# Convolutional attention kernel: attention product kept apart from the output projection

## The chip, the cores and the metric

The kernel runs on one NeuronCore of a Trainium2 chip. The metric is device time in microseconds of one execution. The kernel before takes 750.94 us (median of 3 runs, 750.56 to 751.97).

## The reference, cut to what matters

The input x is (4, 96, 56, 56) in FP32. An attention block and a mixture of four experts are each added to it. Attention has no softmax, so the sum over samples can be done ahead of the queries, as the kernel does; an image has 12 heads of 32 rows.

```python
x = x + conv_attention(layernorm_over_channels(x))
#   value, query: depthwise 3x3, stride 1      key, off: depthwise 3x3, stride 2 (784 places)
#   offset = w_off2 @ gelu(ln(off));  pos = tanh(offset + ref)
#   v_sampled = bilinear sample of value at pos       (784 samples, 96 channels)
#   query, key, v_sampled viewed as (B*NH, HC, pixels) with NH = 12, HC = 32
attn = einsum('bcm,bcn->bmn', query, key) * SCALE
out  = einsum('bmn,bcn->bcm', attn, v_sampled).reshape(B, C, H, W)
y    = einsum('bchw,oc->bohw', out, w_out)
t = tokens(x);  t = t + moe(ln(t))     # 4 experts of 96 -> 384 -> 96, exact gelu, best 2 gates
```

In code the reshape to 12 heads of 32 rows takes 8 channels of 96 for each head and cuts the 3136 pixels of a channel into 4 quarters of 784 (head row = channel in head x 4 + quarter, as it stands in memory). So "channel" means here a pair of a real channel and a quarter, and the 784 samples and keys are cut in the same way: keys have 196 places a quarter.

## The kernel before

Channels are laid on 128 partitions as 4 quarters x 32 channels, in three blocks (BLOCKS = 3, CB = 32): `val`, `query`, `key` and `off` are [128, 3, pixels of a quarter]. The four images go one after the other through a chain. Convolutions are taps on DVE (`tap`, L1133; part of image 0 on PE, L578). Value tokens are stored to a table in memory, POOL gathers sampled rows from it with 16 indirect DMAs an image (`gather`, L1469), and DVE weighs them into `vs` (`sample`, L1335 and L1338). Then comes the part in question.

`key_values` (L632) multiplies samples and keys, one quarter of samples at a time, into [96, 4 x 96]; it waits for one quarter of `vs` each. `mask_kv` (L1348) keeps the entries whose two channels are in the same head. `mixes` (L642) multiplies each masked part by `wout`, three products of 96 columns a quarter; ACT evacuates them to `mix`, [128, 4 quarters, 3 blocks, 96]. `attended` (L662) makes the output, already projected, in 8 steps of 392 pixels: each is three products of `mix` by `query`, summed in PSUM. `add_y` (L1354) on DVE adds it to x. After step n, PE turns x1 of step n-2 to tokens (`x1_to_tokens`, L650), ACT copies them (L826), DVE takes their statistics (`bn`), and the normed tokens go back to channels (`x1_back`, L511) for the experts.

Expert work is cut into chunks of 128 hidden units and 448 pixels, 84 an image, 336 in all. A chunk is three products of FP32R into `ph` (L762 to L764), GELU on ACT (L1006) and one FP32 product into `py` (L746). Three chunks make one output, which DVE scales by its gate into one of four `ye` slots (L1416). POOL issues a DMA that adds it to x for the first 76 (L1480) and adds the later ones itself (L1482); a slot is free when its sum is done. The last 84 chunks are run apart (`last_experts`), with split FP32R products.

The order on each engine is fixed by tables written out by hand or by a planner ahead of time. `CHUNKS_AHEAD` says how many chunks PE has issued before each step of an image, `GELUS_AHEAD` the same for ACT, `OUTPUTS_AHEAD` how many outputs DVE has made at each turn, and `SUMS_AHEAD` how many sums POOL has issued before each of the 8 pairs of gathers. PE, ACT, DVE and POOL run their own instructions strictly in that order. PSUM has two banks for work that ACT evacuates (`pa`) and two for DVE (`pd`); `act_jobs` and `dve_jobs` list their uses in order, and a bank is used again when the job two places before is done.

Of the kernel before, what the change touches and what calls it, by code (L numbers as in the profile page):

```python
# [33 lines left out]
NG = NT // GRP  # L34
# [34 lines left out]
def act_jobs():  # L69

    order = jobs(0, "xT", NG) + jobs(0, "pad", 2 * BLOCKS) + jobs(0, "offT", 2) + jobs(0, "valT", QT)[:VALUE_HALF] + jobs(0, "offc", 2) + jobs(0, "valT", QT)[VALUE_HALF:]
    order += jobs(1, "xT", NG)[:EARLY_SLOTS] + jobs(0, "keyT", 2) + jobs(1, "xT", NG)[EARLY_SLOTS:] + jobs(0, "mix", QUARTERS) + jobs(0, "x1T", NG) + jobs(1, "pad", 2 * BLOCKS)
    order += jobs(0, "gateT", 1) + jobs(1, "offT", 2) + jobs(1, "offc", 2)
    for b in range(1, BATCH):
        more = b + 1 < BATCH
        order += jobs(b, "valT", QT)
        if more:
            order += jobs(b + 1, "xT", NG)
        order += jobs(b, "keyT", 2)
        if more:  # L80
            order += jobs(b + 1, "pad", 2 * BLOCKS)
        order += jobs(b, "mix", QUARTERS) + jobs(b, "x1T", NG)
        if more:
            order += jobs(b + 1, "offT", 2)
        order += jobs(b, "gateT", 1)
        if more:
            order += jobs(b + 1, "offc", 2)
# [27 lines left out]
SCALE_AFTER = 4  # L115
# [3 lines left out]
    dict(x1c=(0, 0, 0, 0, 3, 3, 4), gateT=(3,), offT=(10, 10), offc=(16, 16), offs=(18,)),  # L119
    dict(valT=(42, 42, 43, 43, 44, 44, 45), xT=(45, 46, 46, 47, 47, 48, 48), keyT=(49, 49),  # L120
         pad=(69, 69, 70, 71, 71, 72), kv=(72, 72, 73, 73), mix=(73, 73, 74, 74), y=(74, 74, 74, 74, 74, 74, 74, 74),
         x1T=(74, 74, 74, 74, 74, 74, 75), offT=(75, 76), x1c=(80, 80, 81, 82, 86, 86, 87), gateT=(86,), offc=(93, 93),
         offs=(95,)),
    dict(valT=(118, 118, 119, 119, 120, 120, 121), xT=(121, 122, 122, 123, 123, 124, 124), keyT=(125, 125),
         pad=(145, 145, 146, 147, 147, 148), kv=(148, 148, 151, 151), mix=(151, 151, 152, 152),
         y=(152, 152, 152, 152, 152, 152, 152, 152), x1T=(152, 152, 152, 152, 152, 152, 153), offT=(153, 154),
         x1c=(158, 158, 159, 160, 164, 164, 165), gateT=(164,), offc=(172, 172), offs=(174,)),
    dict(valT=(198, 198, 199, 199, 200, 200, 201), keyT=(204, 204), kv=(222, 226, 233, 233), mix=(233, 233, 234, 234),
         y=(234, 234, 234, 234, 234, 234, 234, 234), x1T=(234, 234, 234, 234, 234, 234, 235),
         x1c=(241, 241, 243, 243, 249, 249, 250), gateT=(249,)),  # L130
# [3 lines left out]
    dict(x1n=(0, 0, 0), x1c=(0, 0, 0, 0, 3, 3, 4), exp=(0,), gateT=(3,), offT=(10, 10), offc=(16, 17), tanh=(19,)),  # L134
    dict(valT=(42, 42, 43, 43, 44, 44, 45), xT=(45, 46, 46, 47, 47, 48, 48), keyT=(49, 49), xn=(67, 69, 69),
         pad=(69, 70, 70, 71, 71, 72), mix=(73, 73, 74, 74), x1T=(74, 74, 74, 74, 74, 74, 75), offT=(75, 76),
         x1n=(78, 80, 82), x1c=(80, 81, 83, 84, 86, 86, 87), exp=(81,), gateT=(86,), offc=(93, 94), tanh=(95,)),
    dict(valT=(118, 118, 119, 119, 120, 120, 121), xT=(121, 122, 122, 123, 123, 124, 124), keyT=(125, 125),
         xn=(143, 144, 145), pad=(145, 146, 146, 147, 147, 148), mix=(151, 151, 152, 152),
         x1T=(152, 152, 152, 152, 152, 152, 153), offT=(153, 154), x1n=(156, 158, 160),  # L140
         x1c=(158, 159, 161, 162, 164, 164, 165), exp=(159,), gateT=(164,), offc=(172, 173), tanh=(175,)),
    dict(valT=(198, 198, 199, 199, 200, 200, 201), keyT=(204, 204), mix=(233, 233, 234, 234),
         x1T=(234, 234, 234, 234, 234, 234, 235), x1n=(239, 241, 243), x1c=(241, 242, 245, 245, 249, 249, 250),
         exp=(243,), gateT=(249,)),
# [43 lines left out]
def build(nc, t, out):  # L188
# [4 lines left out]
    with ExitStack() as ctx:  # L193
# [624 lines left out]
        def _(act):  # L818
# [133 lines left out]
            def first_rest(b, plan, gelus_to):  # L952
# [585 lines left out]
```

## Time and profile before

| | |
|---|---|
| median of the runs | 750.94 us (750.56 to 751.97) |
| profiled execution, span from first to last instruction | 749.4 us; the page gives no other time of it |
| PE busy | 707.8 us, 94% |
| weight loads busy (beside PE) | 495.8 us, 66% |
| DVE busy | 582.8 us, 78% |
| ACT busy | 384.5 us, 51% |
| POOL busy | 216.9 us, 29% |

A product's time in the groups of the page runs from its start to its modelled end, and consecutive products overlap. So the pace of products is read from the chain of waits or from the starts in the timeline, not from their mean. L numbers are lines of the kernel before.

### The profile page before, as it was taken

To read this page: it belongs to the slowest core of one execution; us is meant where nothing else is said; L and a number is where in the kernel's file an instruction comes from. 1 tells how busy PE (TensorE), PEld (TensorE's weight loads), DVE (VectorE), ACT (ScalarE), POOL (GpSimd) and SP (SyncE) were. 2 spreads that over 40 slices of the span, in tenths; PEclk is the share of its full clock that TensorE was granted. 3 is DMA by queue.
4 is the path that set the end of the run, shared out by engine and by line. 5 is a ranking of instruction groups with operands and counts; after the bars stand their busy time and mean duration, and the time that the engine had idled before them with its cause. 6 is when DMAs were issued, how large, how long until landed. Compare 5 with 4: busy or idle time off the path is not lost.

```text
span 749.4 us, 9619 instructions
## 1 busy us (share of the span) xinstructions
PE 707.8 (94%) x3186; PEld 495.8 (66%) x3186; DVE 582.8 (78%) x1511; ACT 384.5 (51%) x722; POOL 216.9 (29%) x184
## 2 busy tenths in 40 slices
PE   5798999799999999999999999999998999999996
PEld 5556566566676666556767566666664665788884
DVE  4889648899999858699999477899975275677774
ACT  2314124744464614744556218545542256899995
POOL 4001700012128610111168201222285121344443
PEclk9998999799999999999999999999999999999999
DMA  8007200044464530345654422435645201121111
GB/s 195 9 0 198 53 9 1 7 98 86 89 185 115 98 56 10 68 103 119 155 129 83 86 48 46 82 80 101 190 102 109 35 20 49 47 69 51 66 47 37
DMA packets 29697, 58.66 MB, mean 78 GB/s; under 512 B 6224, under 2 KB 20176, under 8 KB 29360
## 3 DMA queue, kind: packets, MB, share of 16 engines
q0 software_dynamic: 11584, 17.90, 15.4%
q1 hardware_dynamic: 14336, 32.59, 14.7%
q10 hardware_dynamic: 3728, 7.55, 3.3%
q8 instruction: 26, 0.43, 0.2%
q14 instruction: 23, 0.19, 0.1%
HBM read 30.30 MB, written 14.65 MB: 60 GB/s over the span
## 4 chain that ended last, share of the span: by engine, by line
PE 56%; DVE 19%; DMA 7%; ACT 6%; POOL 5%; issue 5%; POOLq 0%; ACTq 0%
PE py L746 9%; PE pd L662 8%; PE ph L578 7%; DVE val L1133 6%; POOL big L1469 4%; DMA xbuf<-ye 4%; DVE query L1133 3%; PE pa L650 3%; PE pa L529 2%; PE ph L762 2%; PE ph L782 2%; PE ph L784 2%; PE ph L763 2%; PE ph L783 2%; PE ph L764 2%
## 5 line engine op out<-in xcount | busy, mean ns | idle before, releaser
L746 PE MATMUL py<-hid,w 128*96 128x448 f32 x504 | 234.4, 546 | 11.5 <-ACT hid L1006 8.7
L1006 ACT ACTIVATE hid<-ph,b 128x448 f32<-128x448 f32 x252 | 158.9, 632 | 148.1 <-PE ph L764 144.8
L762 PE MATMUL ph<-x_hi,w_hi 96*128 96x448 f32 x252 | 164.4, 653 | 0.0
L1480 POOL DMA_DIRECT2D xbuf<-ye x76 | 66.6, 877 | 327.2 <-DMA xbuf<-ye 163.2
L1469 POOL DMA_INDIRECT big<-value_table,rows x64 | 87.8, 1372 | 90.5 <-DVE rows L1193 56.5
L746 PEld LDWEIGHTS py<-hid,w 128*96 128x96 f32 x504 | 81.6, 165 | 31.2 <-ACT hid L1006 12.6
L763 PE MATMUL ph<-x_lo,w_hi 96*128 96x448 f32 x252 | 93.5, 371 | 0.0
L764 PE MATMUL ph<-x_hi,w_lo 96*128 96x448 f32 x252 | 92.8, 368 | 0.0
L1482 POOL TENSOR_TENSOR xbuf<-xbuf,ye 96x448 f32<-96x448 f32 x36 | 53.9, 1497 | 102.6 <-DVE ye L1416 99.9
L1416 DVE SCALAR_TENSOR_TENSOR ye<-py,b,gate_all 96x448 f32<-96x448 f32 x112 | 75.3, 674 | 9.3 <-PE py L746 7.3
L1443 DVE TENSOR_TENSOR hid_lo<-hid,hid_hi 128x448 fp32r<-128x448 f32 x84 | 59.7, 710 | 27.3 <-ACT hid L1015 27.1
L1133 DVE SCALAR_TENSOR_TENSOR query<-xpad,conv_w,query 128x784 f32<-128x784 f32 x80 | 78.3, 1027 | 0.5
L1133 DVE SCALAR_TENSOR_TENSOR val<-xpad,conv_w,val 128x784 f32<-128x784 f32 x80 | 78.3, 1026 | 0.4
L762 PEld LDWEIGHTS ph<-x_hi,w_hi 96*128 96x128 f32 x252 | 48.3, 192 | 41.1 <-issue 39.7
L763 PEld LDWEIGHTS ph<-x_lo,w_hi 96*128 96x128 f32 x252 | 48.8, 194 | 35.6 <-issue 35.0
L662 PE MATMUL pd<-query,mix_area 128*96 128x392 f32 x192 | 67.2, 493 | 0.0
L1015 ACT ACTIVATE hid_hi<-ph,b 128x448 fp32r<-128x448 f32 x84 | 53.3, 634 | 6.9 <-PE ph L784 1.7
L1015 ACT ACTIVATE hid<-ph,b 128x448 f32<-128x448 f32 x84 | 52.5, 625 | 0.0
L826 ACT ACTIVATE big<-pa 112x400 f32<-112x400 f32 x28 | 14.0, 502 | 70.6 <-PE pa L650 70.6
L764 PEld LDWEIGHTS ph<-x_hi,w_lo 96*128 96x128 f32 x252 | 47.9, 190 | 3.3
L662 PEld LDWEIGHTS pd<-query,mix_area 128*96 128x96 f32 x192 | 29.6, 164 | 23.9 <-issue 23.9
L1354 DVE TENSOR_TENSOR xbuf<-pd,xbuf 96x392 f32<-96x392 f32 x32 | 17.9, 560 | 32.8 <-PE pd L662 32.5
(165 smaller groups left out, 1081.2 us busy)
## 6 DMA issues: line engine op xcount, KB each, us to landing
gate_all<-gate_rows SPq DMA_DIRECT2D x56, 336.0 KB, 3.5
xbuf<-ye POOLq DMA_DIRECT2D x76, 168.0 KB, 3.4
value_table<-valT ACTq DMA_DIRECT2D x6, 1176.0 KB, 8.9
out<-xbuf SPq DMA_DIRECT2D x28, 168.0 KB, 2.0
xbuf<-in_x SPq DMA_DIRECT2D x3, 1176.0 KB, 10.1
value_table<-valT SPq DMA_DIRECT2D x2, 672.0 KB, 5.3
big<-value_table,rows POOLq DMA_INDIRECT x64, 2.8
value_table<-valT SPq DMA_DIRECT2D x2, 504.0 KB, 5.0
```

The lines of the kernel that those rows point to most:

```text
L662: last = nc.tensor.matmul(bank[0:C, 0:YPIX], mix[:, q, i, :], query[:, i, h * YPIX:(h + 1) * YPIX], start=(i == 0), stop=(i == BLOCKS - 1))
L746: nc.tensor.matmul(py[e % 2][0:C, 0:GPIX], w2[:, c, :], hid[:, k % 3, :], start=(j == 0), stop=(j == CPE - 1)).then_inc(hid_used, 1)
L762: nc.tensor.matmul(bank, w1_hi[:, cols], xh(b, g), start=True, stop=False)
L763: nc.tensor.matmul(bank, w1_hi[:, cols], xl(b, g), start=False, stop=False)
L764: nc.tensor.matmul(bank, w1_lo[:, cols], xh(b, g), start=False, stop=True).then_inc(hid_full, 1)
L1006: nc.scalar.activation(hid[:, k % 3, :], ph[k % 2][:, 0:GPIX], ACT.Gelu, bias=b1[:, k % NCH:k % NCH + 1]).then_inc(hid_act, 1)
L1015: nc.scalar.activation(dst[:, k % 3, :], ph[k % 2][:, 0:GPIX], ACT.Gelu, bias=b1[:, k % NCH:k % NCH + 1]).then_inc(ready, 1)
L1133: ins = v.scalar_tensor_tensor(to, src, w, to, ALU.mult, ALU.add)
L1416: v.scalar_tensor_tensor(ye[0:C, e, :], py[e % 2][0:C, 0:GPIX], b2[:, e:e + 1], gate_all[0:C, e, :], ALU.add, ALU.mult).then_inc(ye_ready, 1)
L1443: v.tensor_tensor(hid_lo[:, m % 2, :], hid[:, k % 3, :], hid_hi[:, k % 3, :].bitcast(f32), ALU.subtract).then_inc(hid_lo_ready, 1)
L1469: p.indirect_dma_start(got[:, tile, r, :, :].rearrange("p a c -> p (a c)"), None, table, bass.IndirectOffsetOnAxis(ap=rows[:, r, tile:tile ...
L1480: pool.dma_start(to, ye[0:C, e, :], accum_op=ALU.add).then_inc(ye_summed, 16)
```

## The change

The masked product is no longer multiplied by `wout` ahead of the queries. Keys and samples of each block are multiplied into a full [128, 128] (keys of 4 quarters x 32 channels by samples of 4 quarters x 32 channels), with one mask product on DVE for all three blocks. Six full products of 128 x 128 by 392 query pixels (`attend`) give the attention before projection, with the quarter of the output in the partition group. ACT copies one half of the pixels and DVE the other, 32 rows at a time, from partitions of quarter q to partitions of block i: that makes `att[q]`, 96 channel rows. Three of the four `att` share memory with `val`, the fourth with `offg`. Then each of the 8 steps is one product of `wout` by `att`. Scaling of the next image's tokens in image 0 moves on ACT from after group 4 to after group 6. The waits of DVE on the old products go. `key_values` waits once for all samples. All place tables are new; POOL issues all 16 gathers of an image without a sum between.

```diff
-        order += jobs(b, "mix", QUARTERS) + jobs(b, "x1T", NG)
+        order += jobs(b, "att", BLOCKS) + jobs(b, "x1T", NG)
...
-        order += jobs(b, "kv", QUARTERS) + jobs(b, "y", NY) + jobs(b, "x1c", NG)
+        order += jobs(b, "kv", 1) + jobs(b, "att", BLOCKS) + jobs(b, "y", NY) + jobs(b, "x1c", NG)
...
-         pad=(69, 69, 70, 71, 71, 72), kv=(72, 72, 73, 73), mix=(73, 73, 74, 74), y=(74, 74, 74, 74, 74, 74, 74, 74),
-         x1T=(74, 74, 74, 74, 74, 74, 75), offT=(75, 76), x1c=(80, 80, 81, 82, 86, 86, 87), gateT=(86,), offc=(93, 93),
+    dict(att=(70, 70, 70, 70, 71, 71), gateT=(89,), keyT=(47, 48), kv=(69,), offT=(79, 79), offc=(94, 94), offs=(95,),
+         pad=(65, 65, 66, 66, 67, 67), valT=(44, 44, 45, 45, 46, 46, 47), x1T=(75, 75, 75, 76, 76, 77, 78),
+         x1c=(83, 83, 84, 85, 89, 90, 91), xT=(47, 47, 47, 47, 47, 47, 47), y=(73, 73, 74, 75, 75, 75, 76, 76)),
...
+    dict(att=(231, 231, 231, 231, 232, 232), gateT=(249,), keyT=(211, 211), kv=(230,),
+         valT=(204, 204, 205, 205, 206, 206, 207), x1T=(236, 236, 236, 236, 236, 236, 237),
...
-              (15, 16, 17, 17, 18, 18, 19, 20),
-              (40, 41, 42, 42, 43, 43, 44, 44),
-              (67, 68, 69, 70, 70, 71, 71, 72)]
+              (15, 15, 15, 15, 15, 15, 15, 15),
+              (41, 41, 41, 41, 41, 41, 41, 41),
+              (70, 70, 70, 70, 70, 70, 70, 70)]
...
-        keyT = sb("keyT", [SP, NS, C])
+        keyT = sb("keyT", [SP, 2, BLOCKS, QUARTERS * CB])
+        kv = sb("kv", [128, BLOCKS, QUARTERS, CB])
+        offg = sb("offg", [C, SAMPLES])
+        att = [val[0:C, q, :] for q in range(BLOCKS)] + [offg[:, :]]
...
+            def key_values(b, before=lambda q: None):
+                before(0)
+                pe.wait_ge(sampled, (b + 1) * QUARTERS)
+                bank = dve_bank(b, "kv")
+                for i in range(BLOCKS):
                     for h in range(2):
+                        last = nc.tensor.matmul(bank[:, i * 128:(i + 1) * 128], keyT[:, h, i, :], vs[:, h:NS:2, i * CB:(i + 1) * CB], start=(h == 0), stop=(h == 1))
+                last.then_inc(dve_full, 1)
...
+            def attend(b, before=lambda n: None):
+                pe.wait_ge(query_conv, b + 1)
+                pe.wait_ge(dve_done, dved(b, "kv"))
+                for i in range(BLOCKS):
+                    for h in range(2):
+                        before(2 * i + h)
+                        bank = dve_bank(b, "att", i) if h else act_bank(b, "att", i)
+                        nc.tensor.matmul(bank[:, 0:YPIX], kv[:, i, :, :].rearrange("k q d -> k (q d)"), query[:, i, h * YPIX:(h + 1) * YPIX], start=True, stop=True).then_inc(dve_full if h else act_full, 1)
...
-                    pe.wait_ge(act_done, acted(b, "mix", q))
+                    if n == 0:
+                        pe.wait_ge(act_done, acted(b, "att", BLOCKS - 1))
+                        pe.wait_ge(dve_done, dved(b, "att", BLOCKS - 1))
                     bank = dve_bank(b, "y", n)
-                    for i in range(BLOCKS):
-                        last = nc.tensor.matmul(bank[0:C, 0:YPIX], mix[:, q, i, :], query[:, i, h * YPIX:(h + 1) * YPIX],
-                                                start=(i == 0), stop=(i == BLOCKS - 1))
+                    nc.tensor.matmul(bank[0:C, 0:YPIX], wout[:, :], att[q][:, h * YPIX:(h + 1) * YPIX], start=True, stop=True).then_inc(dve_full, 1)
...
+            def attend(b, i):                                    # ACT
+                bank, full = act_job(b, "att", i)
+                act.wait_ge(act_full, full)
                 for q in range(QUARTERS):
+                    last = nc.scalar.activation(att[q][i * CB:(i + 1) * CB, 0:YPIX], pa[bank][q * CB:(q + 1) * CB, 0:YPIX], ACT.Copy)
+                last.then_inc(act_done, 1)
...
                 for g in range(NG):
                     x1_to_tokens(b, g)
-                    if g == SCALE_AFTER:
-                        scaled(b + 1)
+                scaled(b + 1)
...
-                dve.wait_ge(act_full, acted(b, "mix", QUARTERS - 1))
...
+            def attend(b, turn):                                 # DVE, after mask_kv, before add_y
+                for i in range(BLOCKS):
+                    dve.wait_ge(dve_full, dved(b, "att", i))
+                    for q in range(QUARTERS):
+                        last = v.tensor_copy(att[q][i * CB:(i + 1) * CB, YPIX:QPIX], pd[dve_job(b, "att", i)[0]][q * CB:(q + 1) * CB, 0:YPIX])
+                    last.then_inc(dve_done, 1)
+                    turn()
```

Of the expert outputs, image 1 has 21 made at the last turn of sampling in the new table, 23 in the old; image 2 has 47 and 48.

## Rows read from the trace of the kernel before

**Rows 1.** Page: span, busy time by engine.
```profile
span 749.4 us, 9619 instructions
...
PE 707.8 (94%) x3186; PEld 495.8 (66%) x3186; DVE 582.8 (78%) x1511; ACT 384.5 (51%) x722; POOL 216.9 (29%) x184
```

**Rows 2.** Windows: stretch, length, PE, PEld, DVE, ACT, POOL busy, clock, DMA.
```profile
98.70:142.40 43.70, 38.42 (x200) 25.85 (x198) 30.63 (x130) 20.35 (x51) 0.00 (x0) 0.92 0.00 1
...
204.00:250.00 46.00, 45.88 (x220) 32.50 (x219) 45.17 (x107) 26.04 (x49) 25.77 (x19) 1.00 0.54 136
250.00:305.00 55.00, 53.45 (x269) 35.71 (x267) 38.70 (x139) 25.04 (x55) 10.22 (x12) 1.00 0.28 50
```

**Rows 3.** Chain of waits, image 1: start, length, engine, tile, line, instructions.
```profile
261.78 2.58 PE pd L632 x8
264.36 1.31 PE pa L642 x12
...
268.37 5.93 PE pd L662 x18
274.30 0.78 PE pa L650 x8
```

**Rows 4.** Timeline of PE, two chunks on: start, length, line, operation, idle before.
```profile
241.00 0.92 PE L746 MATMUL py<-hid,w 128*96 128x448 f32 x2
...
242.36 0.92 PE L746 MATMUL py<-hid,w 128*96 128x448 f32 x2
```

**Rows 5.** Groups of DVE by form: busy time, mean ns, idle before.
```profile
L1354 DVE TENSOR_TENSOR xbuf<-pd,xbuf 96x392 f32<-96x392 f32 x32 | 17.9, 560 | 32.8 <-PE pd L662 32.5
...
L1433 DVE CAST w_hi<-w 128x1152 fp32r<-128x1152 f32 x1 | 0.7, 748 | 0.0
```

**Rows 6.** Timeline of DVE in image 0.
```profile
108.63 0.56 DVE L1354 TENSOR_TENSOR xbuf<-pd,xbuf 96x392 f32<-96x392 f32 x1 [4.21 <-PE pd L662]
109.11 1.36 DVE L1082 BATCH_NORM_STATS2 hid<-xT 112x6 f32<-112x96 f32 x8
...
133.21 1.83 DVE L1116 TENSOR_TENSOR big<-big,rstd 112x768 f32<-112x768 f32 x2
```

**Rows 7.** Timeline of DVE in image 1.
```profile
258.58 0.27 DVE L1335 TENSOR_SCALAR key_area<-big,w 98x96 f32<-98x96 f32 x1 [2.29 <-DMA big<-value_table,rows]
...
260.14 1.01 DVE L1348 TENSOR_TENSOR kv_area<-pd,head_mask 96x384 f32<-96x384 f32 x2
...
268.49 1.25 DVE L1130 TENSOR_SCALAR kv_area<-xpad,conv_w,conv_b 128x196 f32<-128x196 f32 x3 [3.54 <-PE pa L642]
...
292.36 0.21 DVE L1059 TENSOR_TENSOR sd<-st 112x28 f32<-112x28 f32 x1
```

**Rows 8.** Timeline of ACT in image 0.
```profile
124.77 3.28 ACT L831 ACTIVATE xT<-xT,hid 112x96 f32<-112x96 f32 x12
...
129.38 0.92 ACT L858 ACTIVATE xpad<-pa 128x392 f32<-128x392 f32 x2 [0.55 <-PE pa L556]
```

**Rows 9.** Timeline of POOL, image 1's gathers: the first, and two together.
```profile
223.27 1.38 POOL L1469 DMA_INDIRECT big<-value_table,rows  x1 [6.28 <-DMA value_table<-valT]
...
240.39 0.96 POOL L1469 DMA_INDIRECT big<-value_table,rows  x1 [0.30 <-issue]
241.66 0.96 POOL L1469 DMA_INDIRECT big<-value_table,rows  x1 [0.30 <-issue]
```

**Rows 10.** Waits of DVE from 404 to 455 us: total, times, longest.
```profile
DVE key_area L1335 <- DMA big<-value_table,rows: 6.3, 2, 3.9
```

**Rows 11.** Chain of waits, image 3's gathers and sums between.
```profile
541.70 2.84 POOL big L1469
544.55 3.57 DMA xbuf<-ye
...
551.37 5.19 DMA xbuf<-ye
...
572.01 2.74 DMA big<-value_table,rows
```

More of the change, by code:

```diff
@@ L71, in act_jobs @@
     order = jobs(0, "xT", NG) + jobs(0, "pad", 2 * BLOCKS) + jobs(0, "offT", 2) + jobs(0, "valT", QT)[:VALUE_HALF] + jobs(0, "offc", 2) + jobs(0, "valT", QT)[VALUE_HALF:]
[L72 removed]
+    order += jobs(1, "xT", NG)[:EARLY_SLOTS] + jobs(0, "keyT", 2) + jobs(1, "xT", NG)[EARLY_SLOTS:] + jobs(0, "att", BLOCKS) + jobs(0, "x1T", NG) + jobs(1, "pad", 2 * BLOCKS)
     order += jobs(0, "gateT", 1) + jobs(1, "offT", 2) + jobs(1, "offc", 2)
@@ L622, in values_to_tokens @@
                     last.then_inc(act_full, 1)
-            def key_values(b, quarters, before=lambda q: None):
-                keyq = keyT[:, :, :].rearrange("p (q h) c -> p h q c", h=2)
-                for q in quarters:
-                    before(q)
-                    pe.wait_ge(sampled, b * QUARTERS + q + 1)
-                    bank = dve_bank(b, "kv", q)
-                    for h in range(2):
-                        last = nc.tensor.matmul(bank[0:C, 0:QUARTERS * C], vs[:, 2 * q + h, :], keyq[:, h], start=(h == 0), stop=(h == 1))
-                    last.then_inc(dve_full, 1)
-            def mixes(b, before=lambda q: None):
-                for q in range(QUARTERS):
-                    before(q)
-                    pe.wait_ge(dve_done, dved(b, "kv", q))
-                    bank = act_bank(b, "mix", q)
-                    for i in range(BLOCKS):
-                        last = nc.tensor.matmul(bank[:, i * C:(i + 1) * C], kv[:, q, i, :, :].rearrange("d k c -> d (k c)"), wout[:, :], start=True, stop=True)
-                    last.then_inc(act_full, 1)
+            def key_values(b, before=lambda q: None):
[3 more added lines that the diff above has]
+                for i in range(BLOCKS):
+                    for h in range(2):
+                        last = nc.tensor.matmul(bank[:, i * 128:(i + 1) * 128], keyT[:, h, i, :], vs[:, h:NS:2, i * CB:(i + 1) * CB], start=(h == 0), stop=(h == 1))
+                last.then_inc(dve_full, 1)
             def x1_to_tokens(b, g):
@@ L858, in padded, with off_to_samples @@
                     nc.scalar.activation(xpad[:, i, r:r + size // W, 1:1 + W], pa[bank][:, 0:size].rearrange("c (h w) -> c h w", w=W), ACT.Copy).then_inc(act_done, 1)
-            def samples(b, name, dst, size, before=lambda h: None):
+            def off_to_samples(b, before=lambda h: None):
                 for h in range(2):
                     before(h)
-                    bank, full = act_job(b, name, h)
+                    bank, full = act_job(b, "offT", h)
                     act.wait_ge(act_full, full)
-                    nc.scalar.activation(dst[:, h:NS:2, :].rearrange("p j (i c) -> p i j c", i=BLOCKS),
-                                         pa[bank][0:SP, 0:BLOCKS * 128].rearrange("p (i j c) -> p i j c", i=BLOCKS, c=CB), ACT.Copy, scale=size).then_inc(act_done, 1)
-            def off_to_samples(b, before=lambda h: None):
-                samples(b, "offT", offT, 1.0, before)
+                    nc.scalar.activation(offT[:, h:NS:2, :].rearrange("p j (i c) -> p i j c", i=BLOCKS),
+                                         pa[bank][0:SP, 0:BLOCKS * 128].rearrange("p (i j c) -> p i j c", i=BLOCKS, c=CB), ACT.Copy).then_inc(act_done, 1)
             def key_to_samples(b, before=lambda h: None):
-                samples(b, "keyT", keyT, SCALE, before)
+                for h in range(2):
+                    before(h)
+                    empty(b, "keyT", h, keyT[:, h, :, :].rearrange("p i k -> p (i k)"), SP, BLOCKS * 128, SCALE)
             def off_gelu(b, before=lambda g: None):
@@ L911, in values_to_tokens @@
                                          pa[bank][0:TP, 0:BLOCKS * 128].rearrange("p (i j c) -> p i j c", i=BLOCKS, c=CB), ACT.Copy).then_inc(act_done, 1)
-            def mixes(b, before=lambda q: None):
+            def attend(b, i):
+                bank, full = act_job(b, "att", i)
+                act.wait_ge(act_full, full)
                 for q in range(QUARTERS):
-                    before(q)
-                    empty(b, "mix", q, mix[:, q, :, :], 128, BLOCKS * C)
+                    last = nc.scalar.activation(att[q][i * CB:(i + 1) * CB, 0:YPIX], pa[bank][q * CB:(q + 1) * CB, 0:YPIX], ACT.Copy)
+                last.then_inc(act_done, 1)
             def x1_to_tokens(b, g):
@@ L986, in rest @@
                     padded(b + 1, lambda g: gelus_to(plan.act_at("pad", g)))
-                mixes(b, lambda q: gelus_to(plan.act_at("mix", q)))
-                act.wait_ge(dve_done, dved(b, "kv", QUARTERS - 1))
+                for i in range(BLOCKS):
+                    gelus_to(plan.act_at("att", i))
+                    attend(b, i)
                 for g in range(NG):
```

73 lines of the change are left out of this document (30 added, 43 removed), and 24 rows, old and new, of the table OUTPUTS_AHEAD.

## The prediction

> **What bounds the kernel now.** I read the page first, then the windows by stage, the chain of waits, and the timelines of PE, DVE, ACT and POOL around one image's attention. The page shows PE busy for 707.8 of 749.4 us and DVE for 78% of it [rows 1]. A busy PE is not yet the bound, so the stages matter. From 204 to 250 us (image 1's convolution taps) PE and DVE are both full: 45.88 and 45.17 of 46 us. From 250 to 305 us (its attention, residual and norm) PE stays at 53.45 of 55, but DVE drops to 38.70 [rows 2]. So before an attention DVE decides and PE is filled with expert chunks; in the attention PE decides and DVE waits. The change cuts PE work where PE decides and adds DVE work there. The question is how much of the cut DVE, or the gathers on POOL, let through.
>
> **PE, part by part.** Every FP32 product is two passes in the trace. By the chain of image 1 [rows 3], 8 passes of 384 columns take 2.58 us (0.322 each), 12 of 96 columns take 1.31 (0.109), 18 of 392 take 5.93 (0.329). Removed per image: keys by values 16 x 0.322 = 5.2, products with wout 24 x 0.109 = 2.6, y 48 x 0.329 = 15.8; together 23.6 us. Added: keys by values 12 passes of 128 columns, 0.133 each on the line between the 96 and 384 column rows, 1.6; six full products 12 x 0.329 = 3.95; y 16 x 0.329 = 5.3; together 10.8. PE saves 12.8 us an image, 38.4 us in images 1 to 3. In image 0 no expert chunk waits to fill PE, so nothing is credited there yet. An expert chunk lasts 1.36 us (the two starts in [rows 4]); that is the price of one step in the new places.
>
> **DVE and ACT.** DVE loses three of four mask products, two of which take 1.01 us back to back [rows 7], so -1.5, and gets 12 copies of 32 x 392 from PSUM. No row shows a copy from PSUM to other partitions. The nearest row is the residual add out of PSUM, also 392 columns: 0.56 us alone [rows 5], 0.48 to the next instruction (108.63 to 109.11, [rows 6]). Below it stands the cast at 748 ns for 1152 columns, SBUF to SBUF, which gives 0.25 us for 392 [rows 5]. I take 0.48, the row with the same source and width: 5.8 us, net +4.3 an image; the ends are 3.0 and 6.7 for the 12. 32 rows in place of 96 save nothing in my sum, since the rows here cost by columns. ACT gets 12 copies at 0.43 (two of 392 columns in 0.92, the first 0.49, [rows 8]), 5.2 us, beside DVE's and shorter than DVE's; its four evacuations of the old products go, uncredited.
>
> Two rules of the Trainium skill bear on this. "VectorE: DVE Perf Modes", section "Why PSUM operands drop a tier", says an FP32 operand in PSUM keeps DVE at its slowest mode; by it the cast's rate is not to be had, and the page's cost line gives an estimate of 0.53 us a copy, 6.4 us in place of 5.8. "TensorEngine Tiling (Array Packing)", section "PSUM Bottleneck", warns that when TensorE gets faster the copies out of PSUM can become the limit, and advises sharing them between ScalarE and VectorE. This change shares them, and the rows agree with the warning: 3.95 us of products against 5.8 of copies. A sum by PE alone would be about 8 us lower than mine.
>
> **Images 1 to 3 along DVE and POOL.** Image 1, to the last sampled row: before at 260.1 us, after a 2.29 us wait for a gather [rows 7]. POOL issues the gathers from 223.27 on, with sums in between; gathers alone follow each other every 1.27 us (240.39 to 241.66, [rows 9]), so 16 in a row take 20.3 us, about 10 less under load, and end ahead of DVE. That wait goes: -2.3. The new output list has two fewer expert outputs ahead of this point (21 against 23), at 0.6 each: -1.2. Then the step that lengthens: one wait for all samples, products 1.6, mask 0.5, two full products 1.3, 12 copies 5.8, one output 0.6, signals 0.7: y begins 10.5 us after the last sample, against 8.2 before (260.1 to 268.37, [rows 3, 7]): +2.3. The new wait of y on both engines' last copies holds all later PE work, but PE has four chunks (69 to 73) put in that gap, 5.4 us. The wait of 3.54 us that DVE had at the first offset tap [rows 7] is swallowed by the copies. From y to the start of the x1 statistics before: 268.49 to 292.36, 23.9 us, of which DVE waits some 5.6, mostly for y. With y at 0.66 in place of 1.98 I leave 1.3 of it: -4.3. Image 1: -2.3 - 1.2 + 2.3 - 4.3 = -5.5.
>
> Image 2 repeats it. DVE's gather waits there are 6.3 us [rows 10]. The new list wants 41 sums ahead of the first gather (before 40), and that sum may still be under way, so I credit 4; outputs -0.8; +2.3 - 4.3 as above: -6.8, together -12.3.
>
> Image 3 has no next image, so DVE is free and POOL decides: gathers and three-chunk sums run from 541.70 to the last landing at 574.75, 33.0 us [rows 11]. Sixteen in a row, 20.3, and the same landing of 2.74 make 23.0: -10. From the last sample (576.2, that landing plus the last sampling) to the last token product the old order has mask and products 8.5, y 15.8, seven groups of 0.78 [rows 3] and one chunk, 31.1. The new one has 1.6 + 3.95 and five chunks (6.8), then y 5.3, groups 5.5 and two chunks (2.7): 25.9: -5.2. It stands then at chunk 237 in place of 235: two chunks done ahead, -2.7. Together -12.3 - 10 - 5.2 - 2.7 = -30.2.
>
> PE agrees: it may save 38.4 and gives back some 8 by waiting for samples ahead of the three key products (between x1 back and there the new places hold 64 chunks where DVE needs the time of about 70).
>
> **Image 0.** DVE is nearly full from the first add at 108.63 to the x1 scaling at 133.21 [rows 6]. The first add comes no earlier (DVE's 12 copies end at about 108), later waits for y go (-2). But the scaling of the next image's tokens on ACT, 3.28 us at 124.77 [rows 8], moves behind all token copies, and PE's padding, which stands ahead of x1 back on PE, waits for it (+2). The granted clock of 98.7 to 142.4 is 0.92 [rows 2], so part of it ran at 1.2 GHz; a PE that idles more there could run y at the lower of its two levels, 1.3 us each, still under DVE's 1.97 a step. I take +1, between -2 and +4.
>
> The two removed waits on the old products cost nothing: taps of the next image now write other memory than the masked products. The last 84 chunks are untouched. The sum is made against the profiled span, 749.4 us, for which the page has no other time; the median is 750.9, so 1.5 us lie around it. 749.4 - 30.2 + 1 = 720.2, and 722 with the 1.5.
>
> **Rivals.** First, the new places hold and PE alone decides: 38.4 less and +1, 713 to 714. For it: PE and DVE met within 1 to 2 us at the old places. Against it: DVE's 45.17 of 46. Chance 0.27. Second, sums starve: with 16 gathers in a row no output is summed for 20 us; the four ye slots and two py banks hold six outputs of three chunks, 24.5 us of PE work, if all are empty when the gathers begin. With two full, PE loses 20.3 - 16.4 = 4, and sums that then land 3.6 to 5.2 us apart [rows 11] against one output per 4.1 us don't catch up: some 5 us in each of three images, 737. Chance 0.15. Third, slower: the copies to other partitions don't stream at the rate of same-partition work. There are 48 on DVE, all between the products and y. At t each they add 48 x (t - 0.48); the 29 us are gone from t = 1.08 us on, and at 1.3 the time is 761. Against it: nothing but the rows' habit of costing by columns. Chance 0.09. Fourth, the change moves work that DVE hides anyway: PE is shortened and every image still takes DVE's time; the gathers' gain is lost too: within 2 us of 751. Chance 0.04; DVE's 16 us of idle time in 250 to 305 speaks against it.
>
> **How the numbers follow.** The forecast, 714 to 731 by the bounds of the copies (3.0 to 6.7, three images), of image 0 and of the gathers, has 0.45. Adding the first rival and most of the second to it gives 709 to 739 for 8 in 10. Faster by over 0.2% (about what can be told from no change): 0.45 + 0.27 + 0.15 and a little of the fourth, 0.87; same 0.03; slower 0.10.
>
> **What would show it.** y as 64 passes in place of 192, and PE's busy time less by 40 to 50; DVE copies of 32 x 392 near 0.5 us; y beginning some 10 us after the last sample; no sum between gathers; PE idle ahead of the key products of images 1 and 2, by 3 to 8 us. I am wrong if a copy costs over 0.8 us, if PE waits for ye, or if PE never waits ahead of the key products (then the first rival).

## The result and the profile after

The changed kernel takes 780.35 us (777.65 to 781.28, four runs) against 750.75 (750.42 to 751.97) beside it: a ratio of 1.038 (95% interval 1.033 to 1.043), slower by 29 us where 29 us less were forecast. Its profiled execution spans 779.5 us at a granted clock of 0.924. Here and below a time is the median of a kernel's runs, and ratios leave out the runs that came in a slower state, among them one of E3 (790.54 us) and one of E7 (765.70 us).

The page after, to be laid beside [rows 1]:

```profile
span 779.5 us, 9244 instructions
...
PE 683.2 (88%) x2994; PEld 486.1 (62%) x2994; DVE 603.7 (77%) x1547; ACT 401.6 (52%) x754; POOL 214.1 (27%) x184
```

PE does less, 683.2 us in place of 707.8, and its share falls from 94% to 88%: work has gone, and PE stands still instead. The waits of PE and then of DVE say where (engine, tile, line, releaser: total, times, longest):

```profile
PE py L739 <- DVE ye L1420: 54.2, 5, 16.6
...
PE pd L657 <- DVE offg L1351: 3.8, 1, 3.8
```

```profile
DVE ye L1420 <- DMA xbuf<-ye: 21.6, 4, 9.5
```

PE waits 54.2 us for DVE to take outputs (`ye`), in five waits, four of them of 6 to 17 us. DVE was late with them: for 21.6 us it waited itself for sums to free a slot, and otherwise its own list had other work first. POOL in image 1 (start, length, line, operation, idle before):

```profile
222.69 0.79 POOL L1484 DMA_DIRECT2D xbuf<-ye  x1 [3.08 <-DMA xbuf<-ye]
235.70 1.99 POOL L1473 DMA_INDIRECT big<-value_table,rows  x1 [12.22 <-DMA value_table<-valT]
...
239.96 4.02 POOL L1473 DMA_INDIRECT big<-value_table,rows  x1 [0.31 <-issue]
...
263.99 0.97 POOL L1473 DMA_INDIRECT big<-value_table,rows  x1 [0.30 <-issue]
264.96 0.98 POOL L1484 DMA_DIRECT2D xbuf<-ye  x1
269.02 0.83 POOL L1484 DMA_DIRECT2D xbuf<-ye  x1 [3.08 <-DMA xbuf<-ye]
```

Between two sums lie 42.3 us (222.69 to 264.96): 12.2 of waiting for the table and 29.3 of gathers, of which single ones took 2 to 4 us. Behind it sums follow each other every 3.9 to 4.1 us, as each waits some 3.08 us for the one before. PE's stop ends 4 us after the first of these sums; the second row is the longest stop, in image 3:

```profile
269.40 1.78 PE L739 MATMUL py<-hid,w 128*96 128x448 f32 x2 [15.28 <-DVE ye L1420]
...
609.67 1.78 PE L739 MATMUL py<-hid,w 128*96 128x448 f32 x2 [16.57 <-DVE ye L1420]
```

The first two-pass product behind the stop takes 1.78 us where it takes 0.92 in [rows 4]: from 269.4 to 272.0 us the granted clock is 0.50. The windows, against [rows 2] (length, then PE, PEld, DVE, ACT, POOL busy, clock, DMA):

```profile
98.70:142.40 43.70, 36.82 (x157) 26.79 (x155) 30.93 (x120) 17.47 (x43) 0.00 (x0) 0.65 0.00 1
204.00:250.00 46.00, 45.27 (x218) 32.38 (x217) 45.65 (x69) 24.00 (x43) 17.05 (x10) 1.00 0.40 105
250.00:305.00 55.00, 38.23 (x169) 25.64 (x168) 36.99 (x130) 23.32 (x48) 18.93 (x21) 0.84 0.38 77
```

From 204 to 250 us both engines are as full as before. From 250 to 305 PE has lost 15 us of busy time, at a clock of 0.84, and in image 0 the clock is 0.65 where it was 0.92. (The changed kernel is some 4 to 20 us later in these windows, so they don't hold quite the same work.)

The copies, which the kernel before doesn't have (DVE, then ACT):

```profile
L1351 DVE COPY val<-pd 32x392 f32<-32x392 f32 x36 | 20.1, 558 | 13.9 <-PE pd L646 13.3
...
L1351 DVE COPY offg<-pd 32x392 f32<-32x392 f32 x12 | 6.8, 568 | 0.2
```

```profile
L911 ACT ACTIVATE val<-pa 32x392 f32<-32x392 f32 x36 | 17.5, 487 | 6.8 <-PE pa L646 6.3
```

For the whole loss I cut the span at marks that the timeline of DVE shows in every image: the x1 scaling, the end of the last value tap, of the last query tap and of the last sample, the start of the first add of y, the end of its last add, the next scaling. Image 2's last three stretches, before and then after:

```profile
418.23 1.46 DVE L1338 SCALAR_TENSOR_TENSOR key_area<-big,w,key_area 98x96 f32<-98x96 f32 x6
...
429.71 0.56 DVE L1354 TENSOR_TENSOR xbuf<-pd,xbuf 96x392 f32<-96x392 f32 x1 [0.66 <-PE pd L662]
...
447.43 0.56 DVE L1354 TENSOR_TENSOR xbuf<-pd,xbuf 96x392 f32<-96x392 f32 x1 [0.56 <-PE pd L662]
...
455.51 1.81 DVE L1116 TENSOR_TENSOR big<-big,rstd 112x768 f32<-112x768 f32 x2
```

```profile
445.99 1.45 DVE L1334 SCALAR_TENSOR_TENSOR key_area<-big,w,key_area 98x96 f32<-98x96 f32 x6
...
466.77 0.55 DVE L1358 TENSOR_TENSOR xbuf<-pd,xbuf 96x392 f32<-96x392 f32 x1
...
480.39 0.55 DVE L1358 TENSOR_TENSOR xbuf<-pd,xbuf 96x392 f32<-96x392 f32 x1
...
487.87 1.81 DVE L1112 TENSOR_TENSOR big<-big,rstd 112x768 f32<-112x768 f32 x2
```

The adds take 14 us in place of 18, but the first comes 19.3 us behind the last sample in place of 10.0. Summed over images 1 to 3 (E4 and E12 to E14 are experiments below; one profiled execution each, us):

| stretch | before | after | E4 | E12 | E13 | E14 |
|---|---|---|---|---|---|---|
| start to the scaling of image 0 | 133.2 | 137.4 | 130.7 | 130.5 | 132.0 | 131.6 |
| scaling to last value tap | 198.7 | 213.1 | 211.5 | 213.8 | 214.7 | 200.1 |
| to last query tap | 102.0 | 102.5 | 107.3 | 116.9 | 102.0 | 102.0 |
| to last sample | 70.7 | 77.9 | 63.2 | 61.0 | 55.1 | 63.4 |
| to first add of y | 30.5 | 56.4 | 50.1 | 50.9 | 54.2 | 34.3 |
| to last add of y | 54.9 | 38.7 | 38.8 | 43.0 | 38.9 | 54.8 |
| to next scaling | 22.5 | 21.4 | 21.3 | 26.5 | 21.3 | 22.5 |
| last scaling to the end | 136.9 | 132.1 | 132.1 | 134.3 | 132.0 | 135.3 |
| span | 749.4 | 779.5 | 755.0 | 776.9 | 750.2 | 744.0 |

The adds give back 16 us, and the stretch ahead of them takes 26; the value-tap stretch takes 14 more and the samples 7.

### The profile page after: what moved, and what is told of

It is laid out like the page before. It is cut to its first block, busy times and chain, and to the rows that moved or that the text cites. A ratio compares the mean times of both kernels' runs of the same rounds, so it can differ in the third digit from the quotient of the medians.

```text
span 779.5 us, 9244 instructions
## 1 busy us (share of the span) xinstructions
PE 683.2 (88%) x2994; PEld 486.1 (62%) x2994; DVE 603.7 (77%) x1547; ACT 401.6 (52%) x754; POOL 214.1 (27%) x184
## 4 chain that ended last, share of the span: by engine, by line
PE 59%; DMA 10%; POOL 9%; DVE 9%; ACT 8%; issue 5%; POOLq 0%; ACTq 0%; DVEq 0%
PE py L739 14%; POOL big L1473 9%; DMA xbuf<-ye 8%; PE ph L574 7%; PE pd L657 3%; PE pa L635 3%; PE ph L755 3%; DVE val L1129 3%; PE ph L756 3%; PE ph L757 3%; PE pa L525 2%; PE ph L775 2%; PE ph L776 2%; PE ph L777 2%; PE py L790 2%
## 5 line engine op out<-in xcount | busy, mean ns | idle before, releaser
L739 PE MATMUL py<-hid,w 128*96 128x448 f32 x504 | 239.6, 557 | 59.8 <-DVE ye L1420 54.2
L1484 POOL DMA_DIRECT2D xbuf<-ye x76 | 63.5, 836 | 371.7 <-DMA xbuf<-ye 192.4
L1420 DVE SCALAR_TENSOR_TENSOR ye<-py,b,gate_all 96x448 f32<-96x448 f32 x112 | 75.5, 675 | 34.8 <-DMA xbuf<-ye 21.6
L635 PEld LDWEIGHTS pa<-ident_gate,xbuf 96*112 96x112 f32 x224 | 31.3, 210 | 12.4 <-issue 9.7
L525 PE MATMUL pa<-ident_gate,xbuf 96*112 96x96 f32 x224 | 30.2, 307 | 7.2 <-DMA xbuf<-in_x 5.2
L1129 DVE SCALAR_TENSOR_TENSOR key_area<-xpad,conv_w,key_area 128x196 f32<-128x196 f32 x96 | 34.8, 418 | 1.0
L1129 DVE SCALAR_TENSOR_TENSOR kv_area<-xpad,conv_w,kv_area 128x196 f32<-128x196 f32 x96 | 34.6, 414 | 0.4
```

Source lines behind the costliest of these rows:

```text
L635: last = nc.tensor.matmul(bank[0:TP, k * XC:(k + 1) * XC], x_of(b)[:, (GRP * g + k) * TP:(GRP * g + k + 1) * TP], ident_gate[:, :], start= ...
L739: nc.tensor.matmul(py[e % 2][0:C, 0:GPIX], w2[:, c, :], hid[:, k % 3, :], start=(j == 0), stop=(j == CPE - 1)).then_inc(hid_used, 1)
L1129: ins = v.scalar_tensor_tensor(to, src, w, to, ALU.mult, ALU.add)
L1420: v.scalar_tensor_tensor(ye[0:C, e, :], py[e % 2][0:C, 0:GPIX], b2[:, e:e + 1], gate_all[0:C, e, :], ALU.add, ALU.mult).then_inc(ye_ready, 1)
L1484: pool.dma_start(to, ye[0:C, e, :], accum_op=ALU.add).then_inc(ye_summed, 16)
```

## The experiments

Ratios are to the kernel before, run beside each on the same chip, with 95% intervals. E1 to E4, E5 to E11 and E12 to E14 ran on three different chips, so between these groups ratios are compared and not times. Letters of theories are those of the expectations: S is that the block of gathers starves the sums, C that the clock falls in image 0's idle time.

**E1, the block undone.** The old list of sums in the changed kernel:

```diff
-              (15, 15, 15, 15, 15, 15, 15, 15),
+              (15, 16, 17, 17, 18, 18, 19, 20),
```

and so for images 2 and 3.

> The changed kernel with one edit: the old list of sums, so that POOL issues sums between the gathers again (15 to 20, 40 to 44, 67 to 72). Theory S (the block of 16 gathers starves the expert sums, ye slots stay full, PE waits for ye): PE's wait for ye falls from 54 us to under 15, the three long gaps of PE (15.3, 13.9, 16.6 us) go, and the time falls by 35 to 50 us, to 730 to 745. Rival A (the new attention itself, its copies and its chain, costs the time, and PE would wait somewhere else): over 765.

763.36 us, 1.016 (1.008 to 1.024): 17 of the 29 us come back, fewer than S had, and the time stays 6 to 18 us over the kernel before. In the profiled execution the stretch to the last sample, in the terms of the table, falls from 77.9 to 60.7 us. PE still waits for `ye`:

```profile
PE py L739 <- DVE ye L1420: 36.3, 6, 14.6
```

**E2, the block alone.** The same edit the other way round in the kernel before.

> The kernel before with one edit: the new list of sums (15, 41, 70 ahead of the first gather, none between). Theory S: the block alone slows the kernel before by 15 to 45 us, to 766 to 796, with PE waits for ye near the gathers of each of images 1 to 3. Rival A: the block is harmless in itself, within 5 us of 751.

793.91 us, 1.054 (1.046 to 1.062). The block by itself costs the old kernel some 41 us; DVE waits 47.8 us for sums there, where it waits 1.1 in the kernel before:

```profile
DVE ye L1416 <- DMA xbuf<-ye: 47.8, 6, 16.9
```

So S is shown as a cause, by taking the block out and by putting it in. It is not the whole, since E1 leaves 1.016.

**E3, the new attention at the old places.** The place tables, output lists and sums of the kernel before, `kv` and `att` where the last old products stood.

> The new attention with the old places (chunks, outputs and sums of the kernel before; the products of keys and values at chunk 72, 148, 229, the six products right behind). Theory S: without the block the attention is a gain, 725 to 748. Rival A: no faster than 751, since the copies hold y and the old places don't fit them; rival P (the new places but for the sums are good): at least 8 us slower than the kernel with the sums between.

787.9 us, 1.041 (1.028 to 1.054), a miss by some 40 us: the old places do not mend the loss. Its windows (PE's busy time first, the clock third from the end):

```profile
275.00:280.00 5.00, 1.06 (x4) 0.29 (x2) 4.85 (x9) 3.03 (x7) 0.79 (x1) 1.00 0.22 54
285.00:290.00 5.00, 5.00 (x19) 3.57 (x19) 3.67 (x13) 1.01 (x2) 0.00 (x0) 0.50 0.02 3
```

With no chunk left between the six products and y, PE stands 4.1 us for DVE's copies (1.06 us busy of 5), and then runs at 0.50, 1.2 GHz, through y and its tokens, though its records show it busy for 5.00 of 5.00 us.

**E4, filler in image 0.** E1, and in image 0 six products ahead of y and one at each step from the third, into a free bank that nobody reads:

```diff
+            def filler(n):
+                for _ in range(n):
+                    nc.tensor.matmul(ph[0][:, 0:YPIX], ident[:, :], query[:, 0, 0:YPIX], start=True, stop=True)
...
-                attended(b)
+                filler(6)
+                attended(b, lambda n: filler(1 if n >= 2 else 0))
```

> The changed kernel with sums between as in the first, and in image 0 filler products on PE (six between the last full product and y, one at each step of y from the third on; their results are not used). Theory C (in image 0 PE idles during the copies, its clock falls to 1.2 GHz, and y and the token products at half rate set the end of that stretch): the granted clock of 98 to 142 us stays above 0.9, x1 comes back 4 to 7 us earlier, and the time is 4 to 7 us under the first. Rival: the copies alone delay it, and the filler changes less than 1.5 us.

759.29 us, 1.010 (1.003 to 1.018), 4 us under E1, at the near end of C's range and with intervals that overlap. The traces are clearer: the x1 scaling of image 0 comes 5.2 us earlier, at 130.70 for 135.91, as C had it, though the clock of 98 to 142 us is 0.88 and not above 0.9. From 105 to 120 us, E1 and then E4:

```profile
105.00:120.00 15.00, 11.21 (x31) 6.38 (x31) 12.01 (x46) 4.23 (x9) 0.00 (x0) 0.63 0.00 0
```

```profile
105.00:120.00 15.00, 14.54 (x66) 8.69 (x64) 13.44 (x61) 3.30 (x7) 0.00 (x0) 1.00 0.00 0
```

Here more work for PE is less time: the clock stays at 1.00 where it was 0.63.

**E5, E3 with filler** in all images, the six into the bank that the next chunk would use:

```diff
+                filler(6)
+
+                def before_y(n):
+                    chunks_to(plan.at("y", n))
+                    filler(1 if n >= 2 else 0)
```

> The new attention at the old places (the third kernel of the first four), with filler products on PE in every image: six between the last full product and y, one at each step of y from the third on; results not used. Theory C (in that kernel PE idles 3.4 to 4.1 us for the copies, its granted clock falls to 1.2 GHz and stays there through y and the token products of each image): the clock of these stretches stays near 1.0, and 20 to 35 us of the 35 us loss come back, 752 to 768. Rival (the time goes to the chain of copies itself, whatever the clock): over 775.

769.76 us, 1.021 (1.014 to 1.029): 18 us under E3, just above the range. The window that stood at 0.50 in E3:

```profile
285.00:290.00 5.00, 5.00 (x29) 3.44 (x29) 5.00 (x19) 1.51 (x3) 0.00 (x0) 1.00 0.00 0
```

So about half of E3's excess over the kernel before was the clock. In the terms of the table the adds take 40.2 us in place of 51.0 and the stretch behind them 22.6 in place of 28.9. The stretch from the last sample to the first add stays at 60.4 (59.9 in E3, 30.5 in the kernel before), which is the rival's part.

**E6, outputs asked for earlier.** E4 with DVE's turns for outputs some positions earlier around the samples, and the scaling on ACT back to after the fifth token copy:

```diff
-                scaled(b + 1)
+                    if g == 4:
+                        scaled(b + 1)
```

> Sums between the gathers and filler in image 0 as in the fourth kernel, with two more edits: DVE's list of outputs brought forward where PE waited for ye (image 1 from 19 to 20, 21 and 22 in the norm and sampling turns, 28 to 29 and 30 near the last x1 turns; image 2 to 46, 47, 48; image 3 to 75 and 76 while sampling), and the scaling of the next image's tokens on ACT back behind the fifth token copy in image 0. Theory O (what was left of PE's wait for ye, 37 us, came of an output list laid down for sums behind the gathers): the wait falls under 15 us and the time by 15 to 25 us, to 735 to 745, under the kernel before. Rival (sums on POOL can't follow whatever the list): the wait stays over 25 us, the time over 752.

766.14 us, 1.017 (1.010 to 1.024): no gain over E4 and perhaps a loss (the intervals overlap), a miss. PE's wait for `ye` fell under 15 us as O had it, but PE's waits only changed their names:

```profile
PE pa L522 <- DVE xT L1093: 15.5, 3, 6.2
PE pd L619 <- DVE key_area L1333: 13.7, 2, 9.9
PE py L737 <- DVE ye L1419: 10.4, 3, 6.7
```

They sum to 39.6 us, against 37.0 for `ye` alone in E4. What DVE does earlier makes something else on it late. Had PE alone set the pace, this should have paid.

**E7 and E8, the price of the copies.** Both on E4, and in both the attention's rows land in the wrong order, so y is not the reference's. E7 copies 128 rows at once in place of 32 rows four times; E8 copies 32 rows to the partitions they come from.

```diff
-                    for q in range(QUARTERS):
-                        last = v.tensor_copy(att[q][i * CB:(i + 1) * CB, YPIX:QPIX], pd[dve_job(b, "att", i)[0]][q * CB:(q + 1) * CB, 0:YPIX])
+                    last = v.tensor_copy(val[:, i, YPIX:QPIX], pd[dve_job(b, "att", i)[0]][:, 0:YPIX])
```

> The fourth kernel with each full product copied as one 128 x 392 block in place of four of 32 x 392, so 3 copies on each of DVE and ACT an image; the turn to channel rows is left out and the attention's values are not those of the reference. Theory K (the four copies stand on the path from the samples to y): y begins some 5 us after the last copy's product earlier, and the time falls by 8 to 20 us over four images. Rival (chunks fill the copies' time): under 4 us.

> The fourth kernel with every 32 x 392 copy written to the partitions it is read from (values not those of the reference). If going to other partitions costs, a DVE copy falls from 0.56 us to 0.48 or less and an ACT copy from 0.49 to 0.41; if 32-row copies cost by their columns alone, both stay within 0.02 us.

E7: 755.64 us, 1.005 (1.001 to 1.009). E8: 754.58 us in a single run. The groups of DVE, E7 and then E8:

```profile
L1355 DVE COPY val<-pd 128x392 f32<-128x392 f32 x12 | 6.8, 567 | 19.6 <-PE pd L646 19.6
```

```profile
L1357 DVE COPY val<-pd 32x392 f32<-32x392 f32 x48 | 26.9, 561 | 11.6 <-PE pd L646 11.0
```

A copy costs the same to other partitions (0.56 us in E4) as to its own, and for 32 rows as for 128. 36 copies fewer, 20 us of DVE's time, are worth some 4 us, which is not clear of the noise (1.005 and E4's 1.010 have intervals that overlap); in the traces the stretch from last sample to first add is 4.0 us shorter in all. DVE waits for PE in place of copying (19.6 in place of 13.4).

**E9 to E11, sums without DMA.** POOL adds every output itself (`BY_DMA = 0` in place of 76), in E4, in the kernel before, and in E6.

> E4 with every output row block added up by POOL itself (about 1.5 us each as its rows show) instead of every second one by an accumulating DMA (0.79 us of issue and a wait of about 3.07 us, 3.87 us a sum, each behind the one before). Theory D (the chain of sums on POOL sets how fast the output path runs, and with it PE's wait for ye): PE's wait for ye falls from 37.0 us to under 15 and the time from 759 to 735 to 750 us. Rival V (VectorE's own list is what is late, and the sums only wait behind it): PE's wait moves to other buffers, the time stays over 755 us.

> The kernel before with the same edit, as the control: its outputs wait for sums for only a few us. Theory D: 745 to 758 us, no clear difference. If it gains as much as E9 does from E4, then the sums are a limit of both kernels and do not explain the loss; if it loses over 5 us, POOL's additions cost VectorE time of their own, and that stands against them in E9 as well.

> E6 (E4 with the outputs asked for earlier) with POOL adding. Theory D: with the sums fast, the earlier outputs cost nothing, 735 to 752 us, not above E9 by more than 3 us. Rival V: VectorE's turns are what is short, as E6's waits for xT norm and key samples said, and it stays 5 us or more above E9.

779.92 us, 1.037 (1.031 to 1.043); 782.03, 1.039 (1.033 to 1.045); 794.22, 1.055 (1.049 to 1.060). Each is slower than the kernel it was made from, by 21, 30 and 28 us, the control as well: so E9 cannot be read for D or against it. E11 against E9, run together, can: both have sums without DMA, and the earlier outputs still cost 14 us, where D allowed 3 and V wanted 5 or more. That speaks for V, with the reserve that POOL's adds slow DVE in both. In E10, DVE (the kernel before first, then E10) and POOL:

```profile
173.40 0.17 DVE L1175 COPY gt<-pz 98x16 f32<-98x16 f32 x1
```

```profile
345.43 1.12 DVE L1175 COPY gt<-pz 98x16 f32<-98x16 f32 x1
```

```profile
345.39 1.12 POOL L1482 TENSOR_TENSOR xbuf<-xbuf,ye 96x448 f32<-96x448 f32 x1 [8.48 <-DVE ye L1416]
350.05 3.75 POOL L1482 TENSOR_TENSOR xbuf<-xbuf,ye 96x448 f32<-96x448 f32 x1 [3.54 <-DVE ye L1416]
```

A copy of 16 columns, 0.17 us in the kernel before, lasts as long as POOL's add beside it; the next add lasts 3.75 us beside three taps. DVE's busy time rises from 582.8 to 627.2 us. The Trainium skill ("SBUF — State Buffer", section "SBUF: two separate sides") says that a VectorE instruction in a mode with two ports, or with two inputs from SBUF, and a GpSimd instruction hold a shared pair of ports as an exclusive lock, for the whole instruction; these rows agree. One thing E9 does show: DVE waits only 3.3 us for slots there, and PE still waits 49.8 us for `ye`, so a late DVE alone, here one slowed by POOL, is enough for that wait.

**E12, the chain cut short.** E4 with no chunk between y and the token copies of images 1 to 3, and the later places called earlier (image 1 here; output lists to match):

```diff
-y=(73, 73, 74, 75, 75, 75, 76, 76), x1T=(75, 75, 75, 76, 76, 77, 78), x1c=(83, 83, 84, 85, 89, 90, 91)
+y=(73, 73, 73, 73, 73, 73, 73, 73), x1T=(73, 73, 73, 73, 73, 73, 74), x1c=(78, 78, 79, 80, 84, 85, 86)
```

> E4 with other places: in images 1 to 3 no chunk stands any more between the products of y and the token copies behind them (in E4 three to five, 1.37 us each), what comes behind them is called five chunks earlier, and VectorE's output list follows. Theory K (the length of an image is the chain of VectorE from the x1 scaling through value taps, gathers, samples and attention to the next x1 scaling, 36 us from the last sample to the scaling in the kernel before and 36 us in E4; TensorE's saved time lies beside it): the stretch from the last sample to the scaling falls from 36 to 29 to 33 us in images 1 and 2, and the time from 759 to 738 to 752 us. Rival P (the outputs' path is the limit, wherever the chunks stand): the same chunks press on the sums elsewhere, and the time stays at 756 us or above.

778.49 us, 1.032 (1.025 to 1.039), a miss:

```profile
275.00:280.00 5.00, 3.31 (x9) 1.06 (x8) 4.89 (x12) 1.32 (x3) 0.79 (x1) 1.00 0.06 11
285.00:290.00 5.00, 5.00 (x19) 3.58 (x19) 3.83 (x14) 1.01 (x2) 0.00 (x0) 0.50 0.12 34
```

The same picture as in E3: a short stop, then 1.2 GHz through y, whose adds take 43.0 us in place of 38.8. In E4, with chunks in y's stage, the same window stays at 1.00:

```profile
285.00:290.00 5.00, 5.00 (x34) 3.88 (x34) 5.00 (x19) 1.64 (x3) 0.73 (x1) 1.00 0.06 19
```

So these chunks, like E5's filler, keep the clock up there. The query-tap stretch grows by 9.6 too, where DVE now waits for PE's late outputs (23.8 us over the run, 9.5 in E4), which is my output list and no finding.

**E13 and E14, gathers that need not wait.** Images 1 to 3 gather from image 0's value table, in E4 and in the kernel before; both leave out that an image attends to its own values. Their own tables are still written, elsewhere, and DVE waits for them ahead of the gates.

```diff
-                    pool.wait_ge(table_out, 32 * (b + 2))
+                    pool.wait_ge(table_out, 64)
```

> E4, but images 1 to 3 gather from the value table of image 0, their own tables being written to memory that nobody reads: left out is that they attend to their own values. So the gathers don't wait for the image's value taps and table (POOL waits 25.8 us for it in E4, 15.0 in image 3). Theory K: the samples end sooner behind the query taps, 17 to 24 us in E4 to 8 to 16, and the time falls to 735 to 752 us. Rival P: sums and outputs are what PE waits for, 755 us or above.

> The kernel before with the edit of E13 and the same part left out. Theory K (VectorE's chain set the length of an image in the kernel before as well, so that what TensorE saves can't count there): its samples, 22 to 26 us behind the query taps, end 8 us or more sooner, and the time falls by 8 to 25 us, to 727 to 744 us. Rival T (TensorE, 94% busy, bounds the kernel before, as the prediction had it): 746 to 753 us.

E13: 751.12 us, 0.996 (0.993 to 0.999), under E4's 1.010 and at the end of K's range. E14: 749.34 us, 0.996 (0.993 to 0.999), 3 us under the kernel beside it and inside T's range. So the wait for the table is not what holds the kernel before: its samples end 7 us sooner in all, and the stretch behind them grows by 4, since `kv` stands behind chunks that TensorE has not reached. Its windows in E14 have no idle time:

```profile
200.00:230.00 30.00, 30.00 (x163) 22.48 (x163) 29.65 (x51) 17.12 (x32) 12.60 (x9) 1.00 0.63 164
230.00:265.00 35.00, 35.00 (x153) 23.11 (x152) 28.75 (x97) 18.55 (x39) 21.44 (x19) 1.00 0.49 103
```

In E4 TensorE idles (its longest wait of the whole run):

```profile
PE py L745 <- DVE ye L1426: 37.0, 6, 16.2
```

There the last chunk ahead of the keys of image 3 (PE), and DVE at that time:

```profile
585.22 1.78 PE L745 MATMUL py<-hid,w 128*96 128x448 f32 x2 [16.16 <-DVE ye L1426]
586.79 2.77 PE L627 MATMUL pd<-key_area,keyT 98*128 98x128 f32 x12
```

```profile
582.84 0.27 DVE L1337 TENSOR_SCALAR key_area<-big,w 98x96 f32<-98x96 f32 x1 [3.45 <-DMA big<-value_table,rows]
583.02 1.46 DVE L1340 SCALAR_TENSOR_TENSOR key_area<-big,w,key_area 98x96 f32<-98x96 f32 x6
584.40 0.67 DVE L1426 SCALAR_TENSOR_TENSOR ye<-py,b,gate_all 96x448 f32<-96x448 f32 x1
```

The wait bears the name of `ye`, but the key products right behind it need the sample that ends at 584.5. So nearly all of PE's 16 us would be lost to the samples if not to `ye`.

How far the two kernels differ is less clear than the medians make it. In the profiled executions of the table E13 shortens E4's span by 4.8 us and E14 the kernel before's by 5.4, and in both the stretch ahead of the first add takes 4 us of it back. That the chain of DVE decides in E4 and TensorE in the kernel before fits all these rows; that what TensorE saves can't count in E4 for this reason is argued and not shown.

## Why the prediction was wrong

Laid on the marks of the table, the forecast and what came of it, as change against the kernel before (us):

| term of the prediction | forecast | after | E4 |
|---|---|---|---|
| image 0 | +1 | +4.2 | -2.5 |
| value and query taps, images 1 to 3 | none | +14.9 | +18.1 |
| gathers (-2.3, -4, -10) and two lists of outputs (-1.2, -0.8), to the last sample | -18.3 | +7.2 | -7.5 |
| last sample to y, images 1 and 2 | +4.6 | +15.1 | +9.6 |
| y and what is behind it, images 1 and 2 | -8.6 | -9.4 | -9.4 |
| image 3 from its last sample to its scaling | -5.2 | +2.7 | +2.3 |
| behind the last scaling | -2.7 | -4.8 | -4.8 |

**The step that failed** is the gathers' gain: -16.3 for 16 gathers in a row. It was worked out from 1.27 us a gather and 20.3 us in all, and the block then had no price beyond the second rival's 5 us an image. In image 1 the block takes 29 us behind a wait of 12 for the table, and 42 pass between two sums; E2 prices it at some 41 us on the old kernel, E1 at 17 here. The rival had the right mechanism and the wrong size: it let the silence of the sums begin with the first gather and last 20 us, where they stop at the wait for the table and the gathers themselves take longer. The prediction's own sign of error, "if PE waits for ye", is the row of 54.2 us. E1 leaves 1.016, so this step explains 17 of the 58 us between 722 and 780.

**The step from the last sample to y** failed second. It was given +2.3 an image; it took 5.8 and 9.3 more in images 1 and 2, and in E4, where `kv` begins with the last sample, still 4.7 and 4.9 (14.9 in place of some 10 us to the first add): products, mask, the six products, copies at 0.57 and the chunks put between. In image 3 the same step ate the gain of -5.2. The credit for y itself held: -4.3 was forecast, and adds and path behind them took 4.7 less, with 16 passes an image in place of 48. In this form the attention moved PE's work out of the adds and put a longer chain of products, copies and signals ahead of them: over three images 88.9 us from last sample to last add in E4, for 85.4 before.

**The taps** were put at nothing, and that failed as well. In E4 the value taps take 12.8 us more, and 11 of these are idle time of DVE (17.6 us before, 28.6 in E4); its own work there is 182.9 us for 181.1, outputs 26.7 for 25.7 of it. It waits longer for ACT's `x_hi`, ahead of the experts (12.2 us for 7.9), and for PE's outputs (5.9 for 1.4). With the old places and lists this stretch takes 203.0 us (E3) and 204.6 (E5), 4 to 6 more than before, so the new places account for 7 to 8 of the 12.8. The 5.3 us more of the query taps are waits for sums in image 3, the longest 4.5 us.

**PE's 12.8 us an image** should have taken some 50 us from its busy time. 24.6 went, 30.7 in E4, where the prediction's own sign was 40 to 50; part of the rest is that products took longer at the lower clock. What went shortened the adds, and the chain ahead of them took it back. That PE and DVE are both full in the tap stretch was read off [rows 2]; what I did not draw from it is that a saving on one of two full engines is worth nothing past the point where the other decides. E14 fits a kernel before that TensorE bounds, but by little. My fourth rival ("every image still takes DVE's time") is nearest to E4.

**Image 0** was given +1 between -2 and +4; its scaling came 4.2 us later (137.41 against 133.21 in [rows 6]). The term named the clock but held that y at 1.2 GHz would stay under DVE's step, and that the copies would end at about 108. They end at 111.4, PE stops 3.8 us for them, and the first add comes 4.5 us late (108.63 in [rows 6]):

```profile
113.10 0.56 DVE L1358 TENSOR_TENSOR xbuf<-pd,xbuf 96x392 f32<-96x392 f32 x1 [1.73 <-PE pd L657]
```

E4 holds the clock there, has its first add at 108.87 and its scaling at 130.7.

**The copies** were sized a sixth too low, 0.48 for 0.56 to 0.57: 6.7 us an image, the upper end of the range. The third rival, slow copies to other partitions, is out by E8. The rule of "TensorEngine Tiling (Array Packing)", section "PSUM Bottleneck", in the Trainium skill, that copies can become the limit when TensorE gets faster, is borne out only weakly: E7 removes 36 of 48 DVE copies and gains some 4 us, not clear of the noise.

**What stays open.** Whether any set of places brings the new attention below the kernel before: none of the runs with all the work in it is one; E4, at 1.010 (1.003 to 1.018), is nearest. Which of the new places makes DVE wait in the value taps was not tested apart. Whether the sums' rate or DVE's turns would be next once the block is gone is not settled either, because E9's edit costs DVE time.

## What to carry to other kernels

Before crediting an engine's saved time, cut one period at marks on the engine that waits, and ask which of these stretches gets shorter: work taken from one of two full engines can leave the period where the other holds it. Before moving transfers into a block, find everything that queues behind them on the issuing engine, and count its silence from the last service ahead of the block, waits included. And where a stage loses its dense products, try other products in it: in E4 and E5 they held the clock at 1.00.

## What the hardware showed that was not expected

TensorE ran at 0.50, 1.2 GHz, while its records show it busy for 5.00 of 5.00 us (E3, E12), after a stop (3.9 us idle of 5 in E3, 1.7 in E12) and with only y and token products behind it; with expert chunks (E4) or filler (E5) among them it stayed at 1.00. A copy out of PSUM cost 0.56 us on DVE and 0.49 on ACT for 392 columns, for 32 rows as for 128, to whichever partitions. A DVE copy beside an addition on POOL lasted as long as that: 0.17 us became 1.12 (E10).
